# AdaLN block with Koopman attention: the known blocks of the Schur squares and of the inverse are added by GpSimd instead of by mask products on TensorE

## The reference

```python
G = Kc.T @ Kc + RIDGE_EPS * I            # 64 x 64
W = jnp.linalg.solve(G, Kc.T @ Vc)
U = U0                                    # first 8 columns of I
for _ in range(POWER_K):                  # twice
    U, _ = jnp.linalg.qr(W @ U)
Wr = U @ (U.T @ W)
S_new = DECAY_ALPHA * S + Wr              # S runs over the chunks of a head
out = SCALE * (Qc @ S_new)
```

## Time and profile before

| | us |
|---|---|
| median of 3 runs (1574.62 to 1580.41) | 1578.5 |
| the profiled execution's own time | 1578.29 |
| its span | 1576.5 |
| TensorE busy / weight loads / VectorE busy | 994.5 / 792.3 / 1293.8 |
| ScalarE busy / GpSimd busy | 650.0 / 225.0 |
| mask products L826, 256 records | 90.0 |

### The profile page before, as it was taken

How to read it: one execution, slowest core, us unless ns; L and a number is a source line. 1 busy time by engine, 2 the same in 40 slices (tenths; PEclk the granted TensorE clock), 3 DMA queues, 4 the chain that set the end, 5 groups by cost and what they waited for, 6 DMA issues and landing times.

```text
span 1576.5 us, 48154 instructions
## 1 busy us (share of the span) xinstructions
PE 994.5 (63%) x19646; PEld 792.3 (50%) x19646; DVE 1293.8 (82%) x3840; ACT 650.0 (41%) x1366; POOL 225.0 (14%) x149
## 2 busy tenths in 40 slices
PE   1344910596276789777789876773474832997165
PEld 1333510464265667666667665662463721776144
DVE  5884589859998779899779799889489789889677
ACT  3563610264143456543456543452242520664032
POOL 3551001101102001302001302001500000001200
PEclk9555965698589899988889988897687975999577
DMA  2555100011000001110001110012220200210000
GB/s 73 174 174 181 30 25 0 2 29 41 1 4 3 4 10 44 39 59 4 4 6 47 32 53 3 4 37 81 66 72 1 72 16 0 78 31 24 9 14 23
DMA packets 52109, 61.94 MB, mean 39 GB/s; under 512 B 4048, under 2 KB 32416, under 8 KB 51888
## 3 DMA queue, kind: packets, MB, share of 16 engines
q1 hardware_dynamic: 51888, 58.84, 12.1%
HBM read 38.31 MB, written 20.51 MB: 37 GB/s over the span
## 4 chain that ended last, share of the span: by engine, by line
PE 46%; DVE 26%; issue 10%; ACT 5%; POOL 2%; DMA 1%; POOLq 0%; SPq 0%; DVEq 0%; ACTq 0%
PE a_bank L688 6%; DVE a_blocks L1561 5%; DVE a_outer L1553 5%; PE a_bank L826 5%; PE a_bank L759 4%; PE a_bank L933 4%; PE a_bank L816 3%; PE a_bank L832 3%; PE a_bank L702 3%; PE a_bank L914 3%; PE a_bank L948 3%; PE a_bank L884 2%; PE a_bank L777 2%; PE a_bank L787 2%; ACT a_work L1076 1%
## 5 line engine op out<-in xcount | busy, mean ns | idle before, releaser
L1553 DVE TENSOR_TENSOR a_outer<-a_blocks 128x512 f32<-128x512 f32 (+19 forms) x608 | 308.9, 541 | 11.7
L1561 DVE TENSOR_TENSOR a_blocks<-a_blocks,a_outer 128x512 f32<-128x512 f32 (+19 forms) x608 | 303.7, 532 | 0.8
L1076 ACT ACTIVATE a_work<-a_bank 128x512 f32<-128x512 f32 (+1 forms) x193 | 110.3, 602 | 215.7 <-PE a_bank L798 174.3
L1466 POOL TENSOR_TENSOR a_root<-a_recip,a_half 128x32 f32<-128x32 f32 (+2 forms) x24 | 91.6, 3819 | 699.0 <-DVEq L1576 692.2
L798 PE MATMUL a_bank<-a_ident,a_blocks 128*128 128x128 f32 x256 | 36.5, 311 | 167.2 <-DVE a_blocks L1612 165.6
L1076 ACT ACTIVATE a_solve<-a_bank 128x512 f32<-128x512 f32 (+2 forms) x184 | 87.9, 523 | 108.1 <-PE a_bank L832 50.2
L688 PE MATMUL a_bank<-a_wk,a_cg 128*128 128x512 f32 x256 | 121.2, 619 | 0.0
L798 PEld LDWEIGHTS a_bank<-a_ident,a_blocks 128*128 128x128 f32 x256 | 35.4, 201 | 167.9 <-DVE a_blocks L1612 125.9
L1076 ACT ACTIVATE a_xb<-a_bank 128x512 f32<-128x512 f32 x112 | 63.5, 597 | 90.6 <-PE a_bank L933 54.1
L1076 ACT ACTIVATE a_scaled<-a_bank 128x512 f32<-128x512 f32 (+1 forms) x130 | 65.4, 530 | 78.0 <-PE a_bank L816 68.1
L816 PE MATMUL a_bank<-a_solve,a_work 32*32 32x64 f32 x4096 | 58.2, 247 | 62.3 <-issue 49.0
(11 more groups left out here) (197 smaller groups left out, 2236.1 us busy)
## 6 DMA issues: line engine op xcount, KB each, us to landing
f_x<-in_L_attn_x SPq DMA_DIRECT2D x16, 256.0 KB, 3.1
s_xnt<-f_xt SPq DMA_DIRECT2D x16, 256.0 KB, 2.1
s_c<-f_cm SPq DMA_DIRECT2D x16, 256.0 KB, 2.3
s_base<-f_base SPq DMA_DIRECT2D x16, 256.0 KB, 2.8
a_cg<-s_c SPq DMA_DIRECT2D x16, 256.0 KB, 2.8
a_cc<-s_c SPq DMA_DIRECT2D x16, 256.0 KB, 3.9
a_xnt<-s_xnt SPq DMA_DIRECT2D x16, 256.0 KB, 3.9
a_base_in<-s_base SPq DMA_DIRECT2D x13, 256.0 KB, 2.6
```

Source lines behind the costliest of these rows:

```text
L1076: nc.scalar.activation(out, view, ACT.Copy, scale=scale).then_inc(emptied, 1)
L1466: nc.gpsimd.tensor_tensor(root[:, :, a:b], recip[:, :, a:b], half[:, :, a:b], ALU.pow).then_inc(roots_ok, 1)
L1553: return ch.inc(V.tensor_tensor(product, bcast(column, 2, area.shape[2]), bcast(row, 3, area.shape[3]), ALU.mult))
L1561: return ch.inc(V.tensor_tensor(area, area, product, ALU.add))
```

## The change

`squares` loses the mask, the known block and the choice of half: its products start each region themselves. ScalarE writes the squares of `schur` to `kept` and to a new region `rest` (in `solve`), and sets a flag after each lot of 32 pairs. GpSimd's `complement(g)` adds `rest` to `gram`, 128 partitions by 32x32 elements, in four pieces; TensorE's `to_problems` waits for all four. In `assemble`, GpSimd's `inverse(g)` subtracts `kept` from the corner of `pair`, in four lots of two pieces (32 partitions by 32x32 elements, one per problem half); the first `apply_inverse` of `subspace` waits lot by lot, and `kept_free` waits for all.

On GpSimd, `complement(g)` stands between the two root steps and ahead of `lengths(g - 1)`, and `inverse(g + 1)` ahead of `combine(g)`. At the end the order is roots and `complement` of group 3, `hidden.pool(0)`, `inverse(3)`, `hidden.pool(1)`, `combine(2)`, `hidden.pool(2)`.

`xa` and `xb` become the two halves of `rest`; the feed-forward weights are quantised in `pair`, so the wait for their store moves from `subspace` to `assemble`. Two small tiles `ga1`, `ga2` take the gates that used the masks' tiles.

```diff
-        solve = sb("solve", [P, 2 * NQ * HB + 2 * HB])
+        solve = sb("solve", [P, 3 * NQ * HB + 2 * HB])
-        minus = [sb(f"minus{h}", [P, P]) for h in range(2)]
+        rest = solve[:, 2 * NQ * HB + 2 * HB:].rearrange("p (q c) -> p q c", c=HB)
-        xa, xb, xc = (sb(n, [P, T, D]) for n in ("xa", "xb", "xc"))
+        xa, xb = (rest[:, NQ // 2 * i:NQ // 2 * (i + 1)].rearrange("p q c -> p (q c)").rearrange("p (t d) -> p t d", d=D) for i in range(2))
+        xc = sb("xc", [P, T, D])
-        w_rows, w_tmp = xb[:].rearrange("p t d -> p (t d)"), xc[:].rearrange("p t d -> p (t d)")
+        w_rows, w_tmp = pair[:].rearrange("p q c -> p (q c)"), xc[:].rearrange("p t d -> p (t d)")
...
+        def apart(first, second):
+            return bass.AP(first.tensor, first.offset, [first.ap[0], first.ap[1], [second.offset - first.offset, 2], first.ap[2]])
...
             def kept_free(self):
-                self.u.need(self.u.mark())
+                self.pe.wait_ge(inverse_ok, G * (NQ // 32))
                 self.pe.sem_inc(kept_read, 1)
...
-            def squares(self, k, half, mask, known):
+            def squares(self, k):
                 four = self.u.fill(4, apart=True)
-                for c in range(4):
-                    at = 32 * k + 8 * c
-                    nc.tensor.matmul(four[c][:].rearrange("p (q z c) -> p q z c", z=2, c=HB)[:, :, half], mask[:], known[:, at:at + 8, :],
-                                     start=True, stop=False, skip_group_check=True)
...
-                            last = nc.tensor.matmul(four[c][rows(s, None), i * DH:(i + 1) * DH], both, both, start=False, stop=True,
-                                                    skip_group_check=True)
+                            last = nc.tensor.matmul(four[c][rows(s, None), i * DH:(i + 1) * DH], both, both, start=True, stop=True)
...
-                    m = self.squares(k, 1, minus[1], gram)
-                straight(self.to_problems(gram, m))
+                    self.squares(k)
+                self.pe.wait_ge(complement_ok, g * (NQ // 32) + NQ // 32)
+                straight(self.to_problems(gram, self.u.mark()))
...
                 def products(k):
+                    if made is not None:
+                        self.pe.wait_ge(inverse_ok, made + k + 1)
...
-            def solved(self, dst, scale=1.0):
+            def solved(self, dst, done, scale=1.0):
...
                     self.squares(k, dst, scale)
+                    self.flag(done)
             def schur(self, g):
-                self.solved(halves.rearrange("p z q c -> p q z c"), -1.0)
+                self.solved(lambda at: apart(kept[:, at:at + 8], rest[:, at:at + 8]), squares_ok, -1.0)
...
             def assemble(self, g):
-                self.solved(pair[:].rearrange("p q (z c) -> p q z c", z=2))
+                self.act.wait_ge(ffn_w_saved, 16 * (2 * NW + 1))
+                self.solved(lambda at: pair[:, at:at + 8].rearrange("p q (z c) -> p q z c", z=2), sums_ok)
...
-                roots(1)
-                roots(2)
-                with pool.Fori(0, G - 1) as g:
-                    roots(g * 2 + 3)
-                    lengths(g)
-                    roots(g * 2 + 4)
+                def complement(g):
+                    for k in range(NQ // 32):
+                        at = slice(32 * k, 32 * k + 32)
+                        pool.wait_ge(squares_ok, g * (NQ // 32) + k + 1)
+                        nc.gpsimd.tensor_tensor(gram[:, at], gram[:, at], rest[:, at], ALU.add).then_inc(complement_ok, 1)
+                def inverse(g):
+                    for k in range(NQ // 32):
+                        at = slice(32 * k, 32 * k + 32)
+                        pool.wait_ge(sums_ok, g * (NQ // 32) + k + 1)
+                        for s in range(2):
+                            corner = pair[rows(s, 0), at, 0:HB]
+                            done = (corner_ok, inverse_ok)[s]
+                            nc.gpsimd.tensor_tensor(corner, corner, kept[rows(s, 0), at], ALU.subtract).then_inc(done, 1)
+                            pool.wait_ge(done, g * (NQ // 32) + k + 1)
+                def upto_schur(g):
+                    roots(g * 2 + 1)
+                    complement(g)
+                    if not isinstance(g, int) or g:
+                        lengths(g - 1)
+                    roots(g * 2 + 2)
+                upto_schur(0)
+                inverse(0)
+                with pool.Fori(0, G - 2) as g:
+                    upto_schur(g + 1)
+                    inverse(g + 1)
                     combine(g)
-                for n in range(G - 1):
-                    hidden.pool(pool, n)
+                upto_schur(G - 1)
+                hidden.pool(pool, 0)
+                inverse(G - 1)
+                hidden.pool(pool, 1)
+                combine(G - 2)
+                hidden.pool(pool, 2)
                 lengths(G - 1)
...
```

More of the change, by code:

```diff
@@ L590, in main_pass @@
         xnt = [sb(f"xnt{i}", [P, NC, D]) for i in range(GB_N)]
-        base_in, ga = sb("base_in", [P, NC, D]), sb("ga", [P, 1, D])
+        base_in, ga, ga1, ga2 = sb("base_in", [P, NC, D]), sb("ga", [P, 1, D]), sb("ga1", [P, 1, D]), sb("ga2", [P, 1, D])
         nhalf = sb("nhalf", [P, GB_N, NC])
@@ L601, in main_pass @@
         schur_in, schur_out = sem("schur_in"), sem("schur_out")
+        squares_ok, complement_ok, sums_ok, corner_ok, inverse_ok = (sem(n) for n in ("squares_ok", "complement_ok", "sums_ok", "corner_ok", "inverse_ok"))
         basis_in, basis_out = sem("basis_in"), sem("basis_out")
@@ L637, in main_pass @@
         bases = [base_in[:], base1, base2, base3]
-        gas = [ga[:]] + [m[:].rearrange("p (u d) -> p u d", u=1) for m in minus] + [ga3]
+        gas = [ga[:], ga1[:], ga2[:], ga3]
         small = [c[:].rearrange("p c d -> p (c d)") for c in cg]
@@ L873, in assemble @@
                     self.u.need(marks[k], apart=True)
-                    self.squares(k, 0, minus[0], kept)
+                    self.squares(k)
             def moments(self, src, mark):
@@ L920, in up_to_model, with apply_inverse @@
                 return mark
-            def apply_inverse(self, src, mark, via):
+            def apply_inverse(self, src, mark, via, made=None):
                 self.u.need(mark, apart=True)
                 def products(k):
+                    if made is not None:
+                        self.pe.wait_ge(inverse_ok, made + k + 1)
                     two = self.u.fill(2, apart=True)
@@ L958, in subspace @@
                 m = yield from self.down_to_heads(wk, xa, m)
-                m = yield from self.apply_inverse(ya, m, xb)
+                m = yield from self.apply_inverse(ya, m, xb, g * (NQ // 32))
                 m = yield from self.up_to_model(wvt, yb, m)
@@ L1142, in squares @@
                     bank = self.u.empty()
-                    self.move(dst[:, at:at + 8], bank[:].rearrange("p (q z c) -> p q z c", z=2, c=HB), scale)
-            def solved(self, dst, scale=1.0):
+                    self.move(dst(at), bank[:].rearrange("p (q z c) -> p q z c", z=2, c=HB), scale)
+            def solved(self, dst, done, scale=1.0):
                 self.scale_rows(0)
@@ L1207, in subspace @@
             def subspace(self, g):
-                self.act.wait_ge(ffn_w_saved, 16 * (2 * NW + 1))
                 yield from self.tiles(xa)
@@ L1671, in finish @@
                     V.tensor_tensor(y, y, x, ALU.add).then_inc(done_ok, 1)
-                for tile in minus:
-                    last = V.memset(tile[:], 0.0)
-                ch.link(last)
                 dve.wait_ge(ident_ok, 2)
@@ L1679, in _ @@
                         at = rows(s, h)
-                        V.tensor_scalar(minus[h][at, at], ident[at, at], -1.0, None, ALU.mult)
                         for eye in eyes:
```

1 line of the change is left out of this document (removed).

## The result

| | before | after |
|---|---|---|
| median us | 1576.56 (4 runs) | 1636.94 (4 runs, 1635.54 to 1640.09) |
| ratio, 95% interval | | 1.0386 [1.0353, 1.0419] |
| profiled execution / span | 1578.29 / 1576.5 | 1637.82 / 1636.0 |
| `quantise(0)` starts | 1199.71 | 1264.95 |

The change costs 60 us. 1627 was predicted, with a range of 1580 to 1645.

A forecast was written before the change was run, and what follows sets the result against it. Main-pass rounds were taken as a relay, VectorE's lead factors nearly binding TensorE's `lead_return`. Walks +32.9, `schur` 0, clash -1.9 and last group +17.9 made +48.9 us on 1578.3: 1627 us, range 1580 to 1645.

The forecast's parts named there:

- The leads: VectorE's three lead factors: eight GpSimd corner pieces hold VectorE 2.0 us each, plus `combine`: 16, 18 and 18 us longer.
- The slack: Before TensorE's `lead_return`: VectorE has only 10.7, 6.1 and 2.3 us to spare; anything added beyond that moves the end.
- `schur` at 0: TensorE's four `schur` stages: 2.6 us gained from missing records, lost to waiting for the last `complement` piece; net 0.
- No gain from 90 us of products: Solve stages: code loading at 3.7 us per 127 records binds; removal gives 2.6 in `schur`, 3.3 in `assemble`, worth nothing.
- Rival (a): Solve stages: the products' 11.25 us leave each stage whole, VectorE slowed as forecast; 1609 us; chance 12%.
- The last group: Last Schur factor to `quantise(0)`: 98.1 us instead of 80.2, +17.9, as SP's weight rows wait behind `combine(2)`.
- The clash at L1643 and L1644: VectorE's L1611/L1612 in the kernel before: slowing beside `combine(2)` in the last group goes away, 1.9 us gained.
- ScalarE's earlier wait for the weights' store: Before `assemble(0)`: booked at 0, since the store is issued before VectorE's first Schur factor.
- (b): Lead factors: 32-partition pieces don't slow VectorE, code loading binds; 1581 us, no change; chance 13%.
- (c): Solve stages: 11.25 us leave each and reach the end, corner pieces costing VectorE under about 0.6; 1535 us; chance 9%.
- (d): GpSimd's adds take up to 4 us instead of 2.5, `products` wait, VectorE loses 24 us a lead; about 1650; chance 6%.
- the signs named: Leads about 103 us or more, `lead_return` idle 7 to 20, solve stages 26 to 28, FFN-row idle over 30, among others.

The follow-up runs named there:

- the four kernels of the table: Kernel before; kernel after; kernel before without mask products (1558.6 us); kernel after with 16 idle 128x256 products put back per solve stage (1646.0 us).

## Why the prediction was right, step by step

The direction and the mechanism that decides, VectorE held by the corner pieces, are shown. That the total came within 10 us has luck in it: 13.6 us came back that were not booked (7.6 behind the Schur factors' starts and 6 at the end), and without them it would have been about 1651, above the stated range.

**The leads: right, and shown.** 16, 18 and 18 us were booked, 17.0, 19.1 and 19.0 measured; with the corner pieces out they come back, and with four times the partitions they stay. The value with nothing off for 32 partitions was the right one, 2.1 us a piece for 2.0. The Trainium skill ("GPSIMD Engine Reference", Key points) says that GpSimd contends with VectorE's instructions of two SBUF inputs, with no exception for few partitions; the wide pieces agree with that, at the same 104.6 us.

**The slack: right.** It was used up whole: TensorE now waits at all three (16.4, 22.3 and 14.4 us).

**`schur` at 0: wrong, and the one step that failed.** It came to +5.7, +6.7 and +5.3 us. The wait for the last complement piece was as booked (2.6 us more at `to_problems`, 2.1 to 3.5 by its removal). The 2.6 us that the missing records should have given back came in `schur(0)` (3.1) and in part in `schur(3)` (1.4), but in `schur(1)` and `schur(2)` the stage went from 29.9 and 29.8 to 31.1 and 31.7. The sum had six further lots of 127, each with its gap, behind the first 172 records of such a stage; with the products gone the first gap stands after 107, so it is one lot and one gap more, and the gaps are 1.6 and 1.7 us each. The granted clock, which the argument took as given, fell from 0.83 to 0.55 with the products, but it fell as far in the stages that got shorter. The rest is around the stage: `lead_return`'s transposes, now behind a longer idle of TensorE, take 5.3 to 5.8 us where they took 3.75, and those of `to_problems` 0.8, 0.7 and 2.7 more. In walk 3 the stage got shorter, and these two and the wait make up more than its 5.3. 7.6 of the 17.7 us came back in TensorE's stretch after the Schur factor's start, which wasn't booked either; it ran at the full clock there.

**No gain from 90 us of products: right for this change, by another sum.** Rival (a) wanted 11.25 us off each solve stage; six got 1.4 to 7.9 shorter and two longer. In the stretch from `lead_return` to the Schur factor, leaving the products out of the kernel before gave +3.5, +4.6 and -0.3. The booked gains were 2.6 in `schur` and 3.3 in `assemble`, 24 us in all, and 24 came, but elsewhere: `assemble` got 4.2 to 7.9 shorter (for the 3.3 the prediction shows no working; 27.1 us against its 32 to 35 would have given 5 to 8). In the changed kernel that is worth nothing, as booked, since VectorE ends last before `lead_return`. In the kernel before it is where the gain of leaving the products out came from. The Trainium skill ("Runtime: NRT & Kernel Launch", Instruction fetch mechanics) calls the cost of a block crossing mostly hidden; 14.9 us for 512 records whose execution takes 8.8 says otherwise for streams of small matmuls. The uncut mask products show where it comes nearer: behind long records, three gaps in a stage instead of eight.

**The last group: right.** 18.6 us for 17.9. Its parts: release of the first root 8.6 (8.6 booked), to the second root's input 38.9 (40.6), root 3.5 (3.4), `combine(2)` until SP goes on 24.2 (24.0), xnt 1.9 (2.8), weight rows 5.9 (5.4), to the first gate 16.0 (13.3).

**The clash at L1643 and L1644** went as booked. ScalarE's earlier wait for the weights' store costs nothing that shows; what makes the front of `main_pass` 1.7 us later before the first solve stage was not looked into.

**The other rivals.** (b) and (c) needed leads as short as those of before: out. (d) asked for 4 us a piece; it is 2.67. Of the signs named, solve stages of 26 to 28 us held in six of eight within 0.3 and failed in `schur(1)` and `schur(2)` (31.1, 31.7), and TensorE's idle before `lead_return` (7 to 20) was 22.3 once. The total was 10 us short: 17.7 for `schur`, 3.1 for the leads, 2.3 at the front and 0.7 in the last group, less 7.6 recovered in the walks and 6 at the end.

## What to carry to other kernels

An engine's busy time that stands in a stream of small matmuls may cost much less than it measures (here 24 of 90 us): read first whether the gaps after every so many records would come in its place, and read it in every stage, since two of eight went the other way. Work moved to GpSimd is paid by VectorE in time standing still, by GpSimd's elements per partition and whatever the partitions; on a VectorE that is within 10 us of the path, that is the price. When a block is put into an engine's program, look at who is queued behind it on other engines (here SP's weight rows behind `combine(2)`) and move that first.

## What the runs showed of the hardware beyond that

- A two-input operation of VectorE was held about 2.1 us by a 1024-element piece of GpSimd, even one of 20 elements per partition (2.42 us for it and one of 32, 0.28 for two like them when GpSimd was idle). By total busy time, VectorE loses 1.8 us per corner piece (1381.1 less 1322.4, over 32) and 1.2 per complement piece (1381.1 less 1362.3, over 16), the latter in a stretch with other kinds of operation.
- In the four kernels of the table, solve stages with sixteen 128x256 products had a mean granted clock of 0.70 to 0.88, those without 0.50 to 0.59. Two stages of eight were shorter with the products than without (29.9 and 29.8 against 31.1 and 31.7), six were longer. Eight large products later ran at 5.2 us instead of 3.7.
- In the solve stages every "issue" gap of TensorE ended 2.2 to 3.0 us after a 16.4 KB instruction packet started; with nothing but small matmuls there is one gap to 127 records.
- Cutting a 128x256 product into four of 128x64 at the same columns took a lot from at most 3.9 us (eight records, at the low clock; 2.0 at the full one) to 7.1 (32 records, at the low clock), at 222 ns a record.
